# Attention: the MLP's eight weight loads issued behind the last load of bias rows

## The reference, cut to what matters

```python
q = gconv1x1(bn1(x), qw)
k, v = gconv1x1(kv, kw), gconv1x1(kv, vw)      # kv: x sampled at 8 x 8 points
bias = mlp3(sign(pos) * log1p(abs(pos)))       # (b, heads, 1024, 64)
attn = softmax(einsum('bhid,bhjd->bhij', q * scale, k) + bias, axis=-1)
out = einsum('bhij,bhjd->bhid', attn, v)
x = x + (out_w @ out + out_b)
h1 = gelu(mlp_w1 @ bn2(x) + mlp_b1)            # 512 -> 2048 channels
x = x + mlp_w2 @ h1 + mlp_b2                   # 2048 -> 512
```

## Time and profile before

| what | value |
|---|---|
| median of three runs | 2899.74 us |
| the profiled execution | 2898.61 us |
| its span | 2896.8 us |
| granted TensorE clock, mean share of full speed | 0.974 |
| TensorE matmul busy | 2738.6 us (95%) |
| VectorE busy | 2176.3 us (75%) |
| ScalarE busy | 1650.0 us (57%) |
| GpSimd busy | 100.8 us (3%) |
| DMA moved | 72.21 MB, mean 25 GB/s |

### The profile page before, as it was taken

One profiled execution on the slowest core, in us unless ns is written; L12 is line 12 of the kernel. 1 busy time (PEld: TensorE's weight loads), 2 busy tenths in 40 slices (PEclk: granted clock), 3 DMA queues, 4 the chain that ended last, 5 costly groups with the idle time before them and its releaser, 6 DMA issues. The chain is left out here.

```text
span 2896.8 us, 45091 instructions
## 1 busy us (share of the span) xinstructions
PE 2738.6 (95%) x19977; PEld 1342.3 (46%) x19977; DVE 2176.3 (75%) x1159; ACT 1650.0 (57%) x2588; POOL 100.8 (3%) x65
## 2 busy tenths in 40 slices
PE   7399999999999999999999999999799999999893
PEld 3333333333333333333333333333478888757551
DVE  5499999999999999999999999998542221234447
ACT  2466776767767777677676776766432222211335
POOL 0000000000000000000000000000422000000004
PEclk9699999999999999999999999999899999999997
DMA  1110000100001001000010000000600000200001
GB/s 68 40 38 14 23 22 16 34 14 23 29 11 34 21 16 36 14 23 22 17 34 14 23 29 10 27 5 1 192 1 0 1 0 1 83 0 1 1 1 58
DMA packets 37603, 72.21 MB, mean 25 GB/s; under 512 B 20960, under 2 KB 21920, under 8 KB 35744
## 3 DMA queue, kind: packets, MB, share of 16 engines
q1 hardware_dynamic: 37344, 69.19, 7.4%
q0 software_dynamic: 64, 0.13, 0.0%
HBM read 60.45 MB, written 8.86 MB: 24 GB/s over the span
## 5 line engine op out<-in xcount | busy, mean ns | idle before, releaser
L731 PE MATMUL l_ps<-mlp_w,W2H 128*64 128x512 f16 x8192 | 1369.1, 393 | 20.1 <-DVE mlp_w L760 20.1
L760 DVE TENSOR_TENSOR mlp_w<-words_x,words_y 128x4096 f32<-128x4096 f32 x256 | 1131.3, 4420 | 0.0
L803 ACT ACTIVATE mlp_w<-l_ps 128x512 f32<-128x512 f32 x1024 | 611.0, 597 | 470.2 <-PE l_ps L731 431.1
L731 PE MATMUL l_ps<-mlp_w,W2L 128*64 128x512 f16 x4096 | 804.0, 389 | 0.0
L731 PEld LDWEIGHTS l_ps<-mlp_w,W2H 128*64 128x64 f16 x8192 | 455.3, 108 | 555.0 <-issue 117.4
L748 DVE SCALAR_TENSOR_TENSOR mlp_w<-relu_bottom,sign_ratio,mlp_w 128x2048 f32<-128x2048 f32 x256 | 601.4, 2349 | 109.0 <-ACT relu_bottom L803 106.7
L803 ACT ACTIVATE relu_bottom<-l_ps 128x512 f32<-128x512 f32 x1024 | 613.0, 599 | 71.1 <-PE l_ps L731 1.4
L731 PEld LDWEIGHTS l_ps<-mlp_w,W2L 128*64 128x64 f16 x4096 | 228.9, 109 | 181.4 <-issue 0.7
L706 PE MATMUL l_ps<-mlp_w,W 128*32 128x512 f32 x2048 | 272.8, 605 | 2.1 <-DVE mlp_w L748 2.1
L719 PE MATMUL l_ps<-y_rows,y_weights_halves 12*128 12x512 bf16 x2048 | 202.5, 385 | 12.5 <-DMA y_rows<-y_pieces 12.5
L719 PEld LDWEIGHTS l_ps<-y_rows,y_weights_halves 12*128 12x128 bf16 x2048 | 51.6, 91 | 336.6 <-ACT relu_bottom L803 232.7
(11 more groups left out here) (339 smaller groups left out, 2410.0 us busy)
## 6 DMA issues: line engine op xcount, KB each, us to landing
table_pos<-pos_table SPq DMA_DIRECT2D x64, 512.0 KB, 3.7
mlp_w<-in_mlp_w SPq DMA_DIRECT2D x8, 1024.0 KB, 8.7
X<-in_x SPq DMA_DIRECT2D x8, 512.0 KB, 7.7
bias_scratch<-bias_rows SPq DMA_DIRECT2D x64, 64.0 KB, 2.0
mlp_w_hi<-bias_scratch SPq DMA_DIRECT2D x16, 256.0 KB, 6.7
out<-Q SPq DMA_DIRECT2D x8, 512.0 KB, 2.7
y_rows<-y_pieces SPq DMA_DIRECT2D x192, 12.0 KB
xn_b<-in_out_wT SPq DMA_DIRECT2D x1, 1024.0 KB, 8.4
```

The costliest lines, as they stand in the source:

```text
L731: last = nc.tensor.matmul(out[q][a * DH:(a + 1) * DH, :], w[:, half], h[a][:, :, k], start=False, stop=stop, tile_position=(0, a * DH))
L760: nc.vector.tensor_tensor(hw[i % 3].rearrange("p r (m j) -> p r m j", j=J), words_x.unsqueeze(1).to_broadcast([P, 2, W, J]), words_y[:, 2 ...
L803: nc.scalar.activation((tops, bots)[d][i % 2][:, r, BANK * u:BANK * (u + 1)], banks[BANK_OF[c % PER]][:], ACT.Relu).then_inc(relu, 1)
```

## The change

The eight loads of the MLP's weights leave the loop over groups and get a loop of their own behind it. Order among them, sizes, semaphore and destination are the same.

```diff
                 if g == 1:
                     sp.dma_start(OW, K.dram["out_wT"]).then_inc(ow_in, 16)
+            for g in range(BLK):
                 part = slice(g * FC // BLK, (g + 1) * FC // BLK)
                 sp.dma_start(K.WR[:, part], K.dram["mlp_w"][:, part]).then_inc(K.mlp_in, 16)
```

## The result

The kernel after takes 2892.09 us, the median of nine runs (2890.13 to 2898.31), against 2899.74 us before: a ratio of 0.9975 with a 95% interval of 0.9964 to 0.9985, so 0.25% faster, some 7 us. The profiled execution has a span of 2888.3 us, 8.5 less than before.

What follows compares the result with a forecast made beforehand. The prediction took the first layer's attention stage to be bound by the arrival of bias rows. Group 2 4.9, clock 0.9 and end 0.7 summed to 6.5 us, off 2899.74 giving 2893.2 us; range 2890.5 to 2897.5.

Steps and rivals of the forecast that it cites:

- Group 1's add: VectorE's add of group 1's bias rows: would start at 2052.4 instead of 2054.75 us.
- More: Rival: TensorE at 2.4 GHz from the first product, 8.4 us gained; first pair up to 0.7 earlier, 2890.6 us; chance 0.03.
- Group 2's add: VectorE's add of group 2's bias rows: would start at 2057.1 instead of 2062.04, 4.9 us earlier.
- two weight loads fewer ahead of it: Group 2's bias rows, output weights still in front: landing at 2062.04 - 2 x 2.5 = 2057.0 us.
- To the first product: From group 2's add to TensorE's first L867: 8.3 us as before, so 2065.4, still 4.9 us earlier.
- The clock: TensorE, first product to group 5's add: part of the stretch at 2.4 instead of 1.2 GHz, 0.9 us gained.
- The end: Group 7's add loses its 0.96 us wait for bias rows; 0.7 us reach the end of the stage.
- The cover of the weights: Last weight load lands at 2098, wanted by ACT in the next stage at 2102.5: covered by 4.5 us.
- weights late: Rival: ACT waits ahead of L1004; decides from 3.5 us a load, at 4.9 us costs +4.5 us, 2904.2; chance 0.07.
- Bias pairs land no sooner: Rival: a bias pair by itself needs 4.9 us, the adds stay where they are, 2899.7 us; chance 0.09.
- 5.4 us that I had taken for an empty queue: First bias pair, issue to landing on an empty queue: 5.4 us, used to bound group 2's landing at 2056.6.
- small pieces of the bias loads hold the queue: SyncE's queue: the many small pieces of the bias loads were what held a weight load for 3.65 us.

Runs made afterwards that it cites:

- two_between: Kernel after with the weight loads of groups 0 and 1 put back between the bias loads; 2898.03 us, 0.9994 of the kernel before.
- round_k2: Kernel after with ScalarE's rounding of the output weights moved behind group 1's exponential; two sets, 2890.94 and 2890.17 us, 0.9969 and 0.9967 of before.
- after_c: The kernel after, unchanged, in a third set of runs; 0.9977 of the kernel before.
- late_add8: Kernel after with the weight loads waiting until the last bias rows are added; 2891.98 us, 0.9974 of the kernel before.
- first: Kernel after with all eight weight loads ahead of the first bias load; 2912.97 us, 1.0045 of the kernel before.
- act_queue: Kernel after with the eight weight loads issued on ScalarE's queue at the start of the stage; 2911.11 us, 1.0046 of the kernel before.
- from_g3: Kernel after with one weight load each behind the bias rows of groups 3 to 7, three at the end; 2892.91 us, 0.9971 of before.
- after_again: The kernel after, unchanged, in a second set of runs; 0.9975 of the kernel before.
- late_o6: Kernel after with the weight loads waiting until group 5's product is copied out; 2895.24 us, 0.9982 of the kernel before.
- k2_fill: `round_k2` with seven unread matmuls filling TensorE's idle time ahead of the first transposes; 2890.40 us, 0.9966 of the kernel before.

## Why the prediction was right, point by point

Forecast 2893.2 us, measured 2892.09: a gain of 7.7 by the medians, 7.2 in the stage, against 6.5. The sign, the place and the mechanism were right. That the sum came out so close was in part luck: two terms were off in opposite directions, group 2 by 1.0 us and the clock by 1.7. Times after entry, before and after:

- *Group 1's add*: foreseen 2.4 us earlier; 10.28 to 8.27, 2.0 earlier. The first pair itself lands 0.4 us later, 5.88 against 5.44, where "More" had it up to 0.7 earlier. The pair behind it is now also one of small pieces, and in the 2.5 us from 2046.3 the DMA moved 174 GB/s, against 222 GB/s in the corresponding 2.5 us of before (2047.0 to 2049.5), when a weight load stood behind the first pair. That this delays the first pair is not shown: `two_between`, with a weight load there as before, had 5.76 us, and the kernels with bias rows there 5.62 to 6.12.
- *Group 2's add*: foreseen 4.9 us earlier; 17.57 to 13.64, 3.9 earlier. The step that was mis-sized is "two weight loads fewer ahead of it". The output weights were issued only 4.4 us after entry, held by the second bias pair, and landed 6.9 us later, at 2055.1, 3.5 us behind the second pair and not 2.5. The order was right; the step from the second pair to the output weights took 1.0 us more. The queue's hold, which I had left out there, explains a part: between the bytes of the two the DMA engines were less than half busy for half a microsecond,

```profile
2050.25:2050.75 0.50, 0.00 (x0) 1.00 0.40 103
```

That is 0.3 us. The remaining 0.7 us stay open; the bias pair of group 2, issued at 2050.89, may have taken a share of the engines from the output weights.
- *To the first product*: foreseen 8.3 us behind group 2's add as before; 2065.71 - 2057.40 = 8.31. ScalarE's rounding of the output weights in this chain was read as fixed; `round_k2` shows that it need not be there.
- *The clock*: bounds 0 to 2.7, taken 0.9. In the profile 6.57 us for group 5 (33.20 to 26.63) less 3.94 for the first product (25.89 to 21.95) is 2.6, near the upper bound; 0.9 in `after_c`. The bounds held. In two of three profiles of the kernel after the value near the lower bound was too small. The trace of before had shown the clock back after TensorE had worked from 2070.4 to about 2075.7 without a break, and 3 to 5 us of such work were foreseen ahead of the product. The third profile shows that the same program can also end near 0.9.
- *The end*: foreseen 0.7; 7.20 for the stage less 6.57 is 0.63.
- *The cover of the weights*: foreseen in at 2098 and wanted at 2102.5; measured 2096.7 and 2101.1, a cover of 4.4 against 4.5, and 2.48 us a load against 2.5. The rule of the Trainium skill ("DMA: Bandwidth & Descriptors", section Rules for kernel authors) to issue a DMA early and wait late would have kept the weights in front. The trace does not agree with it for this case: the weights had 4.4 and then 3.7 us to spare (`late_add8` used up the first and 1.6 us of the second at no cost), and the bias rows had none.
- *The rivals*: "weights late" needs 3.5 us a load and had 2.48. "Bias pairs land no sooner": the last load of the second pair was issued at 2047.03 and in 4.6 us later, 2.0 us behind the first pair, with no megabyte between; and over all sixteen bias loads the median to landing fell to 3.9 us (3.1 to 6.0) from 6.7. The 5.4 us that I had taken for an empty queue was long. `first` and `act_queue` show the opposite way what a transfer ahead of the bias rows costs.

## What to carry to other kernels

On one queue, order loads by when their rows are wanted, and ask of each large load what small one stands behind it: here two megabytes ahead of the third group's rows cost most of what eight between the rows had cost (6.4 of 7.2 us of the stage in the profiles, about three quarters by the ratios), and five ahead of later groups cost nothing by the medians and 1.4 us of the stage in one profile. Before a load is moved back, work out its last landing against its first reader, and the reader's reader; that told what could be delayed, and by how much. A second issuing engine was no way around it here: with the weights on ScalarE's queue both queues together moved 406 to 411 GB/s from 2052 to 2066 us, no more than the 426 of `first`, so the transfers share what carries them.

## What the runs showed that was not expected

- A load of small pieces beside a large one on another queue hardly moves: the first bias pair took 26.3 us from entry to use in `act_queue`, as long as when it stood behind all the weights by order (`first`: 2069.76 - 2043.95 = 25.8 us).
- How long an issue holds SyncE's queue depends on what was issued ahead of it. Eight weight loads in a row took 4.43 us (`after`) and 4.69 us (`first`), but one weight load behind two bias loads up to 3.90 us (before). Four bias loads took 4.37 us with nothing ahead (`after`), 19.41 us behind the eight weight loads (`first`) and 22.62 us beside them (`act_queue`). The sentence in the prediction that the small pieces of the bias loads hold the queue fits the first two figures only; what holds it in the other two no run separates.
- TensorE's clock also fell at the start of the next stage in some profiles (`first`, `from_g3`, `after_again`, `late_o6`, both of `round_k2`, `k2_fill`) and not in others (before, after, `after_c`, `act_queue`, `two_between`, `late_add8`). The way from the next stage's first matmul to the MLP's first was 47.3 to 47.5 us with the fall, `late_o6` aside, and 45.9 without: 1.5 us, as much as `round_k2` gains. The row of `after_again`:

```profile
2098.00:2100.00 2.00, 1.52 (x4) 0.54 0.00 0
2100.00:2102.00 2.00, 2.00 (x7) 0.61 0.04 8
```

Ahead of it TensorE had idled 2.4 us between the stages, after a tail of the stage in which it was busy some 70% of the time; in the profile of after it was the same, and the clock stayed. Whether the versions with the rounding moved meet it more often is open: three profiles of three, against four of ten of the others, are too few to say.
